# Fetching rows behind the loop, and the last shared batch among the expert tiles: an attention and expert kernel on one core

## The reference

```python
x = x + _L1_xattn_ref(_layernorm(x, axis=-1), ctx_1024, ctx_1024, ...)
x = x + _L1_ffn_ref(_layernorm(x, axis=-1), ...)
# in _L1_ffn_ref:
shared_out = jnp.einsum('bth,dh->btd', sh, sw3) + sb3          # every token
x_moe = x[index_b, index_t]                                    # 512 tokens
top1_idx = jnp.argmax(expert_scores + exp_bias, axis=-1)       # 1 of 8 experts
z = _ln(jax.nn.silu(h1) * h2, sel_ln_g, sel_ln_b)
out_all = jnp.einsum('meh,edh->med', z, ew3) + eb3
final_out = shared_out.at[index_b, index_t].set(shared_moe_out + expert_moe_out)
```

## Time and profile before

| | |
|---|---|
| Median of 3 runs | 802.12 us (800.11 to 803.22) |
| The profiled execution | 800.4 us, span of its instructions 798.6 us |
| Busy in the span | PE 712.8, DVE 618.7, POOL 379.7, ACT 337.6 us |
| Mean granted clock of TensorE | 0.947 of full speed |
| Chain that ended last | PE 69%, DVE 14%, issue 6%, POOL 5%, ACT 4%, DMA 1% |

### The profile page before, as it was taken

How to read it: one execution, slowest core, us unless ns; L and a number is a source line. 1 busy time by engine, 2 the same in 40 slices (tenths; PEclk the granted TensorE clock), 3 DMA queues, 4 the chain that set the end, 5 groups by cost and what they waited for, 6 DMA issues and landing times.

```text
span 798.6 us, 29128 instructions
## 1 busy us (share of the span) xinstructions
PE 712.8 (89%) x10994; PEld 569.0 (71%) x10994; DVE 618.7 (77%) x1803; ACT 337.6 (42%) x711; POOL 379.7 (48%) x647
## 2 busy tenths in 40 slices
PE   5678469999999999999999999999987999886984
PEld 4557447888888888888888888877665666654763
DVE  4687555788888878887888788887896999887772
ACT  5666323444444434443444444434544555543200
POOL 2788633253545354535453545344343455455334
PEclk9886589999999999999999999999999999999896
DMA  8777500000000000000000000000114223222001
GB/s 284 231 231 228 193 2 2 3 3 2 4 2 3 2 4 3 3 2 3 3 3 3 3 4 3 9 9 23 62 35 121 71 83 95 81 67 70 14 31 56
DMA packets 24655, 40.98 MB, mean 51 GB/s; under 512 B 3855, under 2 KB 16793, under 8 KB 24267
## 3 DMA queue, kind: packets, MB, share of 16 engines
q1 hardware_dynamic: 23096, 37.13, 14.2%
q0 software_dynamic: 704, 1.71, 0.7%
q10 hardware_dynamic: 726, 0.30, 0.1%
HBM read 30.60 MB, written 8.91 MB: 49 GB/s over the span
## 4 chain that ended last, share of the span: by engine, by line
PE 69%; DVE 14%; issue 6%; POOL 5%; ACT 4%; DMA 1%; POOLq 0%; SPq 0%; ACTq 0%; DVEq 0%
PE ps L490 7%; PE ps L484 7%; PE ps L492 6%; PE ps L491 6%; PE ps L684 6%; PE ps L626 4%; DVE mx L1490 4%; PE ps L702 4%; PE ps L740 4%; PE ps L742 3%; PE ps L741 3%; PE ps L628 3%; PE ps L627 2%; PE ps L738 2%; PE ps L618 2%
## 5 line engine op out<-in xcount | busy, mean ns | idle before, releaser
L1107 ACT ACTIVATE pT<-ps 128x1024 f32<-128x1024 f32 x96 | 93.1, 1021 | 125.4 <-PE ps L684 125.4
L1490 DVE TENSOR_REDUCE mx<-ps 128x16 f32<-128x2048 f32 x48 | 109.4, 2279 | 1.0 <-PE ps L645 1.0
L2036 POOL TENSOR_TENSOR y<-y,vec 128x256 f32<-128x256 f32 x32 | 23.2, 724 | 170.7 <-DVE y L1264 170.7
L740 PE MATMUL ps<-xh,w_hi 128*128 128x128 bf16 x512 | 99.4, 219 | 0.0
L741 PE MATMUL ps<-xl,w_hi 128*128 128x128 bf16 x512 | 99.3, 219 | 0.0
L742 PE MATMUL ps<-xh,w_lo 128*128 128x128 bf16 x512 | 99.3, 219 | 0.0
L1948 POOL TENSOR_TENSOR rs<-mv,cst 128x1 f32<-128x1 f32 x132 | 27.7, 210 | 109.8 <-DVE mv L1261 97.2
L1950 POOL TENSOR_TENSOR rs<-rs,cst 128x1 f32<-128x1 f32 x132 | 73.2, 555 | 10.4
L490 PE MATMUL ps<-w_hi,hh 128*128 x256 | 69.8, 273 | 0.0
L492 PE MATMUL ps<-w_lo,hh 128*128 x256 | 69.8, 273 | 0.0
L491 PE MATMUL ps<-w_hi,hl 128*128 x256 | 69.8, 273 | 0.0
(11 more groups left out here) (353 smaller groups left out, 2452.6 us busy)
## 6 DMA issues: line engine op xcount, KB each, us to landing
stage<-in_w SPq DMA_DIRECT2D x32, 384.0 KB, 3.7
vec<-in_vec SPq DMA_DIRECT2D x4, 896.0 KB, 5.2
vec<-in_tw SPq DMA_DIRECT2D x12, 256.0 KB, 2.8
ctxc<-in_ctx SPq DMA_DIRECT2D x19, 128.0 KB, 2.4
comb<-x SPq DMA_DIRECT2D x16, 128.0 KB, 1.7
comb<-x1b SPq DMA_DIRECT2D x16, 128.0 KB, 1.9
out<-x SPq DMA_DIRECT2D x16, 128.0 KB, 2.1
ytok<-t SPq DMA_DIRECT2D x14, 128.0 KB, 1.8
```

Source lines behind the costliest of these rows:

```text
L740: mm(dst, w(w_hi, c, j), xh[:, c, :], start=False, stop=False)
L1107: A(pT[:, 8 * a:8 * a + 8, :].rearrange("p h q -> p (h q)"), ps[:, 2 * a:2 * a + 2, :].rearrange("p g k -> p (g k)"), ACT.Exp, scale=SCALE ...
L1490: nc.vector.tensor_reduce(mx[:, :], att.rearrange("p g s k -> p (g s) k"), AX.X, ALU.max, negate=True).then_inc(m_max, 1)
```

## The change

Four DMAs of SP move from ahead of the loop over batches 4 to 11 to behind it. DVE makes each mask of picks one batch later. On POOL the split of the weight chunk of batch 14 moves into batch 15, behind the affine of `sh_affine`. In the tail the last shared batch is taken up earlier on all four engines, POOL's sums of batches 14 and 15 each move up by one place, and the gather of the shared rows is issued in two halves, at tiles 0 and 1, instead of whole at tile 2.

```diff
@@ SP
+            with sp.Fori(LOOP_C // 2, LOOP_C_END // 2) as i:
+                ... (the loop's body as before)
             sp.dma_start(pos, pos_d.broadcast_to([128, M])).then_inc(row_in, 16)
             sp.wait_ge(d_zero, 1 + 1)
             for b in (B - 2, B - 1):
                 sp.dma_start(ytok_d[b * S:(b + 1) * S, :], zeros).then_inc(d_zeros, 16)
             sp.wait_ge(d_keys, 16 + 16)
             sp.dma_start(key_row, keys_d.broadcast_to([128, M])).then_inc(row_in, 16)
-            with sp.Fori(LOOP_C // 2, LOOP_C_END // 2) as i:
-                ... (the loop's body)
@@ PE
             chosen_hidden(1)
+            sh_out(B - 1, B - 1)
             choice(3)
             chosen_hidden(2)
-            sh_out(B - 1, B - 1)
@@ ACT
             hidden_exp(0)
+            sh_zhi(B - 1)
             choice(2)
-            sh_zhi(B - 1)
@@ DVE
-                if b in (LOOP_C_END, LOOP_C_END + 1):
-                    i = b - LOOP_C_END
+                if b in (LOOP_C_END + 1, LOOP_C_END + 2):
+                    i = b - LOOP_C_END - 1
...
                 last_of_equal(t)
+            sh_sum(B - 2)
+            sh_zlow(B - 1)
             mask_tokens(2)
             gated(0)
-            sh_sum(B - 2)
             gated_norm(0)
+            sh_sum(B - 1)
             mask_tokens(3)
-            sh_zlow(B - 1)
             gated(1)
             mask_z(0)
             gated_norm(1)
             last_of_equal(2)
             gated(2)
-            sh_sum(B - 1)
@@ POOL
-                if weights is not None:
-                    tw(*weights)
+                if b == B - 1:
+                    tw(b - 1 - LOOP_C, (b - 1 - LOOP_C) % 2)
+                if weights and not tokens:
+                    tw(b - LOOP_C, (b - LOOP_C) % 2)
...
             sh_affine(B - 1)
+            sh_sum(B - 2)
...
                 if t == 0:
-                    sh_sum(B - 2)
-                if t == 2:
                     sh_sum(B - 1)
                     pool.wait_ge(s_comb, 16 * B)
                     pool.wait_ge(s_shared, 16 * (B + 1))
-                    gather(range(MT), 0, 2 * D, comb_d, d_gshared)
+                    gather((0, 1), 0, 2 * D, comb_d, d_gshared)
+                if t == 1:
+                    gather((2, 3), 0, 2 * D, comb_d, d_gshared)
```

More of the change, by code:

```diff
@@ L440, in _ @@
             sp.dma_start(keys_d.rearrange("o (p t) -> (o p) t", t=MT), ids[:, 4, :]).then_inc(d_keys, 16)
+            with sp.Fori(LOOP_C // 2, LOOP_C_END // 2) as i:
+                for j in range(2):
+                    put_tokens(i * 2 + (j - 1) if j else (i - 1) * 2 + 1)
+                    put_shared((i - 2) * 2 + j)
+                    next_context(i * 2 + (j + 3))
+                    next_weights((i - 1) * 2 + j, j)
             sp.dma_start(pos, pos_d.broadcast_to([128, M])).then_inc(row_in, 16)
@@ L446, in _ @@
             sp.dma_start(key_row, keys_d.broadcast_to([128, M])).then_inc(row_in, 16)
-            with sp.Fori(LOOP_C // 2, LOOP_C_END // 2) as i:
-                for j in range(2):
-                    put_tokens(i * 2 + (j - 1) if j else (i - 1) * 2 + 1)
-                    put_shared((i - 2) * 2 + j)
-                    next_context(i * 2 + (j + 3))
-                    next_weights((i - 1) * 2 + j, j)
             for b in range(LOOP_C_END, B + 4):
@@ L2074, in sh_sum, with block_c @@
                 tt(fin[:, :], acc[:, :], at(b), ALU.add).then_inc(s_sum, 1)
-            def block_c(b, slot, ex=None, weights=None, tokens=False):
+            def block_c(b, slot, ex=None, weights=False, tokens=False):
                 n = b + UNITS
@@ L2122, in _ @@
                 c = b - LOOP_C
-                block_c(b, b % 2, base_of(UNITS + b - 3) if b < 3 else None, (c, c % 2) if 0 <= c < TCHUNKS else None, b == B - 2)
+                block_c(b, b % 2, base_of(UNITS + b - 3) if b < 3 else None, 0 <= c < TCHUNKS, b == B - 2)
             rstd(1, B - 1 + A1, s_var, s_veps, s_rstd)
```

## The result

| | before | after |
|---|---|---|
| Median of 4 runs each | 801.36 us (800.11 to 803.22) | 790.06 us (787.69 to 790.87) |
| The profiled execution | 800.4 us, span 798.6 us | 790.22 us, span 788.4 us |
| Mean granted clock of TensorE | 0.947 | 0.954 |

The ratio is 0.9852, with a 95% interval from 0.9822 to 0.9882: faster by 11.3 us, where 13.9 had been worked out and 788.2 us predicted. The profiled spans differ by 10.2 us.

A forecast was written before the change was run, and what follows sets the result against it. PE was busiest; the excess lay in long causal beats, DVE's wait at batch 14 and PE's end pauses. Gains 4.58 + 0.75 + 0.75 + 7.8 = 13.9 us off the 802.12 median gave 788.2 us, range 785.5 to 793.

The forecast's parts named there:

- rival 1: End of the kernel: the clock falls in PE's new pause of about 2.5 us, costing 1.80 us, 790.0 us; 17%.
- Part 1: SP's queue at batch 4: fetches behind the loop make two long beats normal, 4.58 us gained; bounds 3.94 and 4.58.
- Part 2: Picks one batch later: the beat of 12.16 falls to 11.41, 0.75 us gained; bounds 0.3 and 0.75.
- Part 3: POOL's weight chunk of batch 14 moved: DVE's wait for the root shrinks, 0.75 us gained; bounds 0.3 and 1.1.
- Part 4: Last shared batch and gather in the tail: tile 2's products start earlier, clock stays up; 7.8 us, bounds 5 and 9.
- the 0.4: Deduction in the tail for late-root spots behind the gathers, half of the 0.9 us found there.
- The term that failed: Tile 2's output products: the upper clock level (2.4 GHz) holds after the shorter PE pause, 1.80 us gained.
- the sign that I had named for it: End of the kernel: a granted clock under 0.9 in the last 10 us would show the forecast wrong.
- Rival 2: Expert tiles: roots late behind the gathers, tile 2's by 0 to 0.9 us; 790, up to 792 us; 13%.
- the paragraph ahead of the sum: Shared-port lock among expert tiles: gathers and roots meet four multiplications; at 0.5 us each, tail gain 6.2, time 789.8.
- Its other part, a late tile 1: Tile 1's root behind landing and gathers: 0.4 us spare; a landing 1 to 2 us longer loses 1 to 2.
- Rivals 3 and 4: 3: batch 4's stall stays, 792.8 us, 5%. 4: keys reach DVE's first mask late, slower than before, 2%.

The follow-up runs named there:

- p2: The kernel before with only the two masks of picks made one batch later; 804.6 us.
- p4: The kernel before with only the edits behind batch 15 on PE, ACT, DVE and POOL (last shared batch earlier, gather in halves); 798.63 us.
- p3: The kernel before with only POOL's weight chunk of batch 14 moved into batch 15; 802.52 us.
- f_end: The changed kernel with unused products in PE's two end pauses, five ahead of tile 2's transpose and seven ahead of tile 3's; 787.26 us.
- g_late: The changed kernel with the second pair of gathers behind tile 2's affine instead of tile 1's; 788.91 us.
- best1: The changed kernel with the last batch's final sum on VectorE, normalizations of tiles 2 and 3 ahead of masks, unused products before their transposes; median 788.90 us.
- f_gate: The changed kernel with five, seven and three unused products in PE's pauses around the gate; 788.18 us.
- d_own: The changed kernel with VectorE instead of GpSimd making the last batch's final sum; 786.87 us.
- f_both: The changed kernel with unused products in PE's pauses at the gate and the end, and the second pair of gathers behind tile 2's affine; 788.49 us.

## Why the prediction held, and where it didn't

The time, 790.06, lies 1.9 us above the forecast, within the range and at the figure of rival 1. That it meets 790.0 so closely is luck: parts 1, 2 and 3 were off by 0.0 to 0.2 us on this pair of profiles, but part 1 is worth 1.6 to 1.8 us more on three others, and the start and the choices move by 2.7 and 1.6 us between executions. By its steps:

- **Part 1** (4.58): 4.56. Both excesses went, and nothing is late in their place: every beat of the loop is 11.41. Two details were wrong. The fetch at 695.45 that I took for the loop's last was batch 12's, behind the loop; the four DMAs went out at 681.37 to 684.07, one batch earlier, taking SP 2.7 us where I had 1.8, in a hole that held them as well: the next store was issued at 685.01, and its follower's 1.94 us of issue kept no one waiting. And the size is that of one execution; p2 to p4 put the wait at 6.2 to 6.4 us with the clock behind it.
- **Part 2** (0.75): 0.55. With the mask gone the beat is 11.61, 0.2 us above the others, and the low half of the gate weights (L1808), for which I had put the lower bound at 0.3, is still in it. It had taken 0.16 us behind the mask, and takes 0.70 now: at 694.25 it starts 0.12 us after an addition of GpSimd (L2019, 694.13, 0.79 us) and ends with it, in the changed kernel as in p2. The same lock as in the tail, with VectorE as the one held, ate 0.54 us of the mask's place; of the 0.2 that are missing this is the likely cause, not tested by itself.
- **Part 3** (0.75): 0.85. The sum for it was made of VectorE's side, with the mask as the last to come. p3 has the same distance without a mask, bound by the root, which waits for its variance and no longer for GpSimd. In the changed kernel both chains end within 0.1 us, since the root's last step is stretched beside the mask, so the size was right and the reason half of it.
- **Part 4** (7.8 = 6.37 + 1.80 - 0.4): 6.74. The start of tile 2's output products came 12.57 - 5.64 = 6.93 earlier behind tile 2's transpose, and that transpose came 0.54 later: 6.39 for the 6.37 less 0.4. The slip was a little more than the 0.4, and 0.4 came back because the mask multiplication that bounds tile 3's root starts 2.08 us behind tile 2's transpose and not 2.49. The root itself ended at 773.82, which is 773.41 plus 0.41, close to the 0.57 that I had let run behind the multiplication. The term that failed is the clock: 0.35 instead of 1.80. I had argued that 2.5 us of pause are too short for it to fall. It was low at 777.5 to 781 behind pauses of 1.24 and 1.70 us, and the sign that I had named for it came: the granted clock of the last 10 us was 0.84, under the 0.9. f_end shows the rest: without the pauses the last two tiles take 6.88, 1.98 less than before.
- **Rival 1** came, in place and in price: 790.0 predicted, 1.45 of its 1.80 us found. Its chance of 17% was too small. The stretch of the earlier trace rows showed only what a long pause did, and I read from it that a short one was harmless, for which no row stood.
- **Rival 2** came at tile 2 (0.54 of 0 to 0.9), and its price there comes from a meeting that its sum doesn't have; the paragraph ahead of the sum has four such meetings at 0.5 us each, where two roots met the multiplication and one of them cost 0.54 on the path. The variance was ready at 764.54, the root started at 765.89, right behind the second gather, and then met the multiplication of 766.17. Started at 764.6 it would have been done by 765.4 by my estimate (0.2 and 0.55 us for its steps), so by the trace the gathers brought the meeting about; no run shows it, since g_late had the slow sum. Taking the meeting away by the exchanged order (best1) gave 0.33. Its other part, a late tile 1, came in four other kernels with the slow sum and cost 0.2 to 0.3 us there, and more behind it in f_gate. The landing and gathers in it were added up 0.2 too high: 758 + 2.5 + 2.7 is 763.2, not 763.4.
- **Rivals 3 and 4** did not: no beat above 11.61, and no wait at a mask.
- **Outside the sum** lay 2.5 us: 1.6 at the start and 1.3 in the choices, less 0.4 at the gate. Both larger ones vary by execution, the choices with the time that the clock is low in them (0.81 against 0.86). Batch 4's maximum starts between 592.2 and 594.9 us in kernels with the same first part: at 592.2 and 592.3 in best1 and d_own, at 594.2 in the changed kernel. The profile of before was at the early end, 592.6, which makes the gain look smaller by spans (10.2) than by medians (11.3).

What stays open: why the start differs between executions, and why the low clock at the gate lasts 10 us in one and 7 in another. In the profile of before it lasted 10 as well (735.2 to 745.4), but began 3.3 us ahead of the choices, so that they had 6.9 of it. The long choices came in after, p4 and best1, all with the new tail, and in none of the four with the old one, but four of seven with the new tail had the short ones too; seven and four profiles don't tell whether the tail has a part in it.

## What to carry over

A wait in a DMA queue costs everything behind it, and moving it behind the loop gave 4.6 us and more for four instructions; that was safe to price from one beat beside its neighbours. A pause that is shortened does not bring the clock back by itself, so a term for the clock belongs in the sum only if the profile shows a pause of the new length with full clock behind it. And where an engine's short step meets another's long one on shared ports, look at what the waiting engine would do instead, and whom the long step meets next, before exchanging them: the stretched root cost 1.1 us; in its place came 0.9 us on the affine and 2.2 us in which VectorE stood idle.

## What the runs showed of the hardware

- The granted clock fell behind pauses of 1.24 and 1.70 us of TensorE, five microseconds apart, and products without a use in these pauses (1.24 and 1.67 us of them) kept it at 1.00 in three kernels. The length of one pause alone doesn't decide: with such products behind it, a further pause of 0.35 and then 1.15 us left the clock up in f_both, and 0.99 and then 0.56 us did not in best1. The products cost nothing where TensorE still had to wait behind them (0.43 and 0.20 us in f_end), and 0.7 us in best1, where the transpose was ready before they ended.
- Two instructions that start 0.04 to 0.07 us apart on VectorE and GpSimd decide 2.1 us of GpSimd's time: 0.72 or 2.84 us for the same sum of 128x256.
- The same root step takes 0.55 us alone and 1.50 to 1.66 beside a bf16 multiplication of 128x2048 with both inputs in SBUF.
- The issue of an indirect DMA by GpSimd takes 0.95 us behind another one, and 1.87 where it began 0.18 us behind a bf16 multiplication of 128x2048 on VectorE.
- The same stall at batch 4 was followed by a low clock of some 3.4 us in one profile and 6.8 in three others, for 1.7 us more.
- The same choices took 24 us where the clock was low for 6.5 to 6.9 us of them, and 25.4 where it was low for 9.3 to 9.7.
